# One decoder layer on one core: weights laid out on the host, an earlier attention, 32 expert homes, and a normalisation shared by VectorE and GpSimd

## The reference, cut to what matters

```
x = x + attn(LN(x));  x = x + cross(LN(x), fside, ctx);  x = x + moe(LN(x))
attn:  fused = h @ w_kv_a -> q_c (192), kv_c (64), k_pe (64)
       q = rms(q_c)*gamma @ w_qb -> 16 heads x (128 nope + 64 rope);  kv = rms(kv_c)*gamma @ w_kvb
       scores = q_full @ k_full^T / sqrt(192), causal; softmax; @ v; @ w_o
cross: SmoothQuant int8 linear with fside (256x256), silu(gate)*up, a second one with ctx (256x128)
moe:   sigmoid router, top 3 of 8 groups, top 4 of 32 experts, capacity 40 slots per expert,
       expert = silu(x@Wg)*(x@Wu)@Wd, weighted sum, plus a shared expert
```

## Time and profile before

| what | value |
|---|---|
| median of three runs | 443.41 us |
| the profiled execution's own time | 444.59 us |
| its span, first to last instruction | 442.8 us |
| TensorE busy | 356.5 us (81%) |
| VectorE, GpSimd, ScalarE busy | 249.4, 209.5, 177.0 us |
| granted TensorE clock, mean | 0.938 |
| chain that ended last: PE, DVE, POOL, issue, ACT, DMA | 39, 20, 10, 10, 8, 8% |
| DMA | 32.14 MB in 45512 packets, 44436 of them under 2 KB |

### The profile page before, as it was taken

How to read it: one execution, slowest core, us unless ns; L and a number is a source line. 1 busy time by engine, 2 the same in 40 slices (tenths; PEclk the granted TensorE clock), 3 DMA queues, 4 the chain that set the end, 5 groups by cost and what they waited for, 6 DMA issues and landing times.

```text
span 442.8 us, 7025 instructions
## 1 busy us (share of the span) xinstructions
PE 356.5 (81%) x2206; PEld 250.0 (56%) x2206; DVE 249.4 (56%) x839; ACT 177.0 (40%) x564; POOL 209.5 (47%) x276
## 2 busy tenths in 40 slices
PE   3299989989999998899898895777677652996980
PEld 2154657656677665675665664565565542553870
DVE  2146464575437686877867976662967660336233
ACT  2123447666616865335774236551132000342000
POOL 3102256676718565359976367742134042000674
PEclk9789999999999999999999999899889685998996
DMA  5999508802000000000000000621000004175353
GB/s 158 206 196 283 169 17 227 242 17 71 1 1 1 0 2 1 0 8 28 7 5 3 1 0 7 179 72 38 0 4 2 19 1 125 48 234 177 89 149 114
DMA packets 45512, 32.14 MB, mean 73 GB/s; under 512 B 8697, under 2 KB 44436, under 8 KB 45348
## 3 DMA queue, kind: packets, MB, share of 16 engines
q1 hardware_dynamic: 42980, 28.45, 24.7%
q0 software_dynamic: 2496, 3.25, 2.9%
HBM read 26.56 MB, written 8.84 MB: 80 GB/s over the span
## 4 chain that ended last, share of the span: by engine, by line
PE 39%; DVE 20%; POOL 10%; issue 10%; ACT 8%; DMA 8%; SPq 4%; POOLq 0%; ACTq 0%; DVEq 0%
PE psum L589 29%; PE psum L598 10%; DMA region_b<-in_L_attn_w_o_dram 3%; POOL expert_rows L1685 3%; DMA region_b<-expert_out,slot_gather 2%; POOL region_b L1699 2%; DVE neg_max L1280 2%; POOL region_t L1653 2%; ACT region_r L974 2%; ACT region_t L1035 1%; POOL rstd L1640 1%; DVE smooth L1341 1%; ACT region_t L974 1%; POOL region_t L1652 1%; SPq L496 1%
## 5 line engine op out<-in xcount | busy, mean ns | idle before, releaser
L589 PE MATMUL psum<-region_h,region_b 128*128 128x256 f32 (+1 forms) x352 | 77.5, 354 | 1.7 <-DVE region_b L1592 1.7
L1652 POOL TENSOR_SCALAR region_t<-region_t,prob_rsums 128x128 f32<-128x128 f32 x64 | 40.9, 639 | 52.2 <-DVE prob_rsums L1274 51.7
L1653 POOL TENSOR_SCALAR region_t<-region_t,prob_rsums 128x256 f32<-128x256 f32 x64 | 64.9, 1013 | 0.0
L1033 ACT ACTIVATE region_t<-psum,neg_max 128x128 f32<-128x128 f32 x64 | 23.8, 372 | 94.5 <-DVE neg_max L1280 94.3
L589 PE MATMUL psum<-region_c,region_h 128*128 128x512 f32 x128 | 61.1, 601 | 0.0
L589 PEld LDWEIGHTS psum<-region_h,region_b 128*128 128x128 f32 x352 | 52.4, 193 | 5.9 <-DVE region_b L1592 2.1
L1699 POOL DMA_INDIRECT region_b<-expert_out,slot_gather x20 | 20.7, 1036 | 48.1 <-DMA expert_out<-region_h 42.3
L1685 POOL DMA_INDIRECT expert_rows<-h_moe,slot_scatter x32 | 33.3, 1042 | 18.4 <-DVE slot_scatter L1528 11.4
L598 PE MATMUL psum<-consts,region_t 128*128 128x128 f32 x192 | 32.0, 275 | 10.6 <-ACT region_t L974 9.9
L598 PEld LDWEIGHTS psum<-consts,region_t 128*128 128x128 f32 x192 | 22.3, 141 | 31.8 <-issue 18.4
L1279 DVE TENSOR_REDUCE neg_max<-psum 128x1 f32<-128x128 f32 x64 | 18.1, 282 | 38.8 <-PE psum L589 38.4
(11 more groups left out here) (204 smaller groups left out, 693.1 us busy)
## 6 DMA issues: line engine op xcount, KB each, us to landing
region_a<-in_L_ffn_W_gate_dram SPq DMA_DIRECT2D x17, 128.0 KB, 2.5
region_a<-in_L_ffn_W_up_dram SPq DMA_DIRECT2D x17, 128.0 KB, 2.6
region_a<-in_L_ffn_W_down_dram SPq DMA_DIRECT2D x17, 128.0 KB, 2.7
region_b<-in_L_attn_w_o_dram SPq DMA_DIRECT2D x2, 1024.0 KB, 13.8
expert_out<-region_h SPq DMA_DIRECT2D x8, 256.0 KB, 3.1
expert_rows<-region_g SPq DMA_DIRECT2D x10, 132.5 KB, 4.2
region_b<-in_L_ffn_W_gate_dram SPq DMA_DIRECT2D x10, 128.0 KB, 2.5
region_b<-in_L_ffn_W_up_dram SPq DMA_DIRECT2D x10, 128.0 KB, 2.5
```

The lines of the kernel that those rows point to most:

```text
L589: return nc.tensor.matmul(out_, lhsT, rhs, start=first, stop=last)
L1033: nc.scalar.activation(probs[:, hn % 4, 0:P], s[:, 0:P], ACT.Exp, bias=nmax[:, hn, 0:1], accum_out=sums[:, hn, 0:1])
L1652: g.tensor_scalar(pr[:, 0:P], pr[:, 0:P], rsum[:, hn, 0:1], None, ALU.mult)
L1653: g.tensor_scalar(pr[:, P:3 * P], pr[:, P:3 * P], rsum[:, hn, 1:2], None, ALU.mult).then_inc(sg["probs_normed"], 1)
```

## The change

- The host lays the weights out: per head the transposed blocks and `w_o` side by side (`fold_w`, four quarters of four heads, 9216 bytes a partition), the rope columns (`rope_w`), `fside` and `ctx` transposed, router and shared weights in one array, each expert as one 128 x 768 block; gammas and bias lie in the constants. `prepT`, `rwT`, `shT`, the transposes of `wx`, and their copies go.
- `prepM` writes two banks, (`prepM`) copied by VectorE and (`mo`) by ScalarE, and forms the [P:QL] part twice, one for each half of the partitions. Only pairs 0 and 1 stand ahead of the heads; six stand in slots 0 to 4.
- `q` handles both tiles of a batch: two full matmuls, then two with 64 rows each, on partitions 0-63 and 64-127. There are four q buffers.
- A slot has a single order, `SLOT`; steps in `SPLIT` have a second mark with "*": TensorE works at the first, the other engines at the second. ScalarE's `exp` of head hn-1 stands in slot hn, VectorE's `max` later in the slot. `BANK_PT` and `BANK_Q` are gone; five banks go round.
- VectorE scales tile 0's probabilities, GpSimd tile 1's. One mask matmul of 256 columns takes the place of two of 128.
- All 32 experts have a home and are loaded once, by one DMA each. The two clamps go.

```diff
-BANK_S, BANK_PT, BANK_O, BANK_Q, BANK_W = 0, 2, 3, 4, 5
+BANK_S, BANK_O, BANK_W = 0, 2, 3
...
-EVEN_SLOT = ("scores", 0, "norm", 1, "q", "probsT", 2, "qT", 3)
-ODD_SLOT = ("norm", "scores", "rope", 0, "probsT", 1, "pv", 2, 3)
...
+SLOT = ("scores", "exp", "*pv", "*q", 0, "rope", "probsT", "max", "norm", 1, "*probsT", "qT", "pv", 2, "q", 3, "*qT")
+SPLIT = ("q", "qT", "probsT", "pv", "hT", "fused", "latT", "prepM", "x_T", "x_back", "x_qT", "x_mm",
+         "x_back2", "x_qT2", "x_mm2", "r_T", "r_logit")
...
+PREP_AT = (0, 1, 5, 7, 12, 16)
+FRONT_AT, FRONT_GAPS, FRONT_NEXT = (20, 40, 54), (0, 2, 5, 8), 4
...
+             ("latents", 0), ("prepM", 0), ("latents", 1), ("latT", 0), ("prepM", 1), ("latT", 1), ("q", 0, 0),
+             ("rope", 0, 0), ("rope", 1, 0), ("qT", 0, 0), ("qT", 1, 0)]
+    for p, at in zip(range(2, 8), PREP_AT):
+        place(at, ("prepM", p))
+    place(3, ("q", 0, 1))
+    place(4, ("rope", 0, 1))
+    place(6, ("qT", 0, 1))
+    place(5, ("ln1_stats", 1))
+    place(6, ("ln1_norm", 1))
...
+def tensor_steps(steps):
+    return [step for step in steps if step[0][0] != "*"]
+def other_steps(steps):
+    later = {step for step in steps if step[0][0] == "*"}
+    kept = [step for step in steps if ("*" + step[0],) + step[1:] not in later]
+    return [(step[0].lstrip("*"),) + step[1:] for step in kept]
...
+                for j in range(NJ):
                     k = ring[n % len(ring)]
                     n += 1
+                    self.at[("q", NJ * step[1] + j, step[2])] = (k, emptied[k], filled[k] + 1, emptied[k] + 1)
+                    filled[k] += 1
+                    emptied[k] += 1
...
+        homes = [r[:, o * WE:(o + 1) * WE] for r, n in ((reg_b, SLOTS_B), (reg_a, SLOTS_A), (reg_c, SLOTS_C)) for o in range(n)]
+        homes += [reg_x[:, :], reg_w[:, 0:WE], reg_w[:, WE:2 * WE], reg_g[:, 3328:3328 + WE]]
+        homes += [reg_f[:, o * WE:(o + 1) * WE] for o in range(4)]
...
+            def load_experts(first, n):
+                for e in range(first, first + n):
+                    sp.dma_start(home(e), expert_w[e]).then_inc(ld_experts[e // XG], 16)
...
+            for c in range(NQ):
+                sp.dma_start(fold[c].rearrange("p h m -> p (h m)"), fold_w[c]).then_inc(ld_fold[c], 16)
+                sp.dma_start(wf[:, c, :, HC * KL:], rope_w[c].rearrange("p (k n) -> p k n", k=2)
+                             ).then_inc(ld_rope_cols[c], 16)
+                if c == 1:
+                    load_x(1)
...
+            load_experts(3, 2)
+            load_experts(9, 1)
+            load_experts(SLOTS_B + SLOTS_A + SLOTS_C, 1)
+            for c in range(NQ):
+                for p in range(2 * c, 2 * c + 2):
+                    wait_filled(sp, ("mo", p))
+                load_experts(SLOTS_B + 3 * c if c < 3 else 0, 3)
             wait_filled(sp, ("fused", NT - 1))
-            for e in range(SLOTS_A + 8, SLOTS_A + SLOTS_B):
-                load_expert(e)
+            load_experts(8, 1)
...
+            load_experts(SLOTS_B + SLOTS_A, SLOTS_C)
             sp.wait_ge(sg["scores_ready"], NHU)
-            for e in range(SLOTS_A + 5, SLOTS_A + 8):
-                load_expert(e)
+            load_experts(5, 3)
+            wait_filled(sp, ("y", NT - 1))
+            load_experts(SLOTS_B + SLOTS_A + SLOTS_C + 1, 3)
+            sp.wait_ge(sg["scaledT_w"], B)
+            sp.wait_ge(sg["scaledT_c"], B)
+            load_experts(E - 4, 4)
...
-            for e in range(NHOME, E):
-                if (e - NHOME) % XG == 0:
-                    wait_filled(sp, ("dn", (e - NHOME) // XG))
-                load_expert(e)
-                if (e - NHOME) % XG == XG - 1:
-                    store_outputs((e - NHOME) // XG)
-            for i in range(2, NG_E):
+            for i in range(NG_E):
...
-                    turn(bank(step)[:, 0:P], wq0[:, h, :])
-                    turn(bank(step)[:, P:2 * P], wkq[:, h, 0:DN])
-                    fills(turn(bank(step)[:, 256:320], wkq[0:KL, h, DN:], ident[0:KL, 0:KL]), step)
...
+                        w = fold[p // 2][:, (2 * p + i) % HC, :]
+                        wkT = w[:, QL:QL + KL]
                         mm_halves(bank(step)[:, i * KL:(i + 1) * KL], w[:, 0:P], wkT)
-                        mm(bank(step)[0:64, 128 + i * KL:128 + (i + 1) * KL], w[:, P + KL:2 * P], wkT)
+                        for half in range(2):
+                            last = mm(bank(step)[half * KL:(half + 1) * KL, 128 + i * KL:128 + (i + 1) * KL],
+                                      w[:, P:QL], wkT)
+                    fills(last, step)
+                    item = ("mo", p)
+                    wait_empty(pe, item)
                     for i in range(2):
-                        last = mm(bank(step)[i * KL:(i + 1) * KL, 256:512], wT[:, (2 * p + i) % 4, 256:320], wo[:, 2 * p + i, :])
-                    fills(last, step)
+                        w = fold[p // 2][:, (2 * p + i) % HC, :]
+                        last = mm(bank(item)[i * KL:(i + 1) * KL, 0:D], w[:, QL + KL:QL + 2 * KL], w[:, QL + 2 * KL:])
+                    fills(last, item)
...
+                    for j, item in enumerate(pair):
+                        wait_emptied(pe, ("latT", NJ * b + j))
+                        wait_empty(pe, item)
+                        mm(bank(item), qn0[:, NJ * b + j, :], wf[:, c, 0, :], True, False)
+                    for j, item in enumerate(pair):
+                        half = slice(j * KL, (j + 1) * KL)
+                        fills(mm(bank(item), qn1[half, b, :], wf[half, c, 1, :], False, True), item)
...
-                    mm(o[:, 0:P], id_bf[:], mask_bf[:], True, False)
-                    mm(o[:, 0:P], q[:, 0:P], kT[:, b, 0:P], False, True)
-                    mm(o[:, P:3 * P], q[:, P:2 * P], kT[:, b, :], True, False)
-                    mm(o[:, 2 * P:3 * P], id_bf[:], mask_bf[:], False, True).then_inc(sg["scores_ready"], 1)
+                    mm(o[:, 0:2 * P], id_bf[:], mask_bf[:], True, True)
+                    nc.tensor.matmul(o[:, 0:P], q[:, 0:P], kT[:, b, P:2 * P], start=False, stop=True,
+                                     skip_group_check=True)
+                    nc.tensor.matmul(o[:, P:3 * P], q[:, P:2 * P], kT[:, b, :], start=False, stop=True,
+                                     skip_group_check=True).then_inc(sg["scores_ready"], 1)
...
+                    pe.wait_ge(sg["probs0_normed"], hn + 1)
                     pe.wait_ge(sg["probs_normed"], hn + 1)
-                    if hn >= 1:
-                        pe.wait_ge(sg["probsT_copied"], hn)
-                    for i in range(3):
-                        last = turn(ps_pt[:, i * P:(i + 1) * P], probs[:, hn % 4, i * P:(i + 1) * P])
-                    last.then_inc(sg["probsT_done"], 1)
+                    wait_empty(pe, step)
+                    for i, block_ in enumerate((0, 2, 1)):
+                        last = turn(bank(step)[:, i * P:(i + 1) * P], probs[:, hn % 4, block_ * P:(block_ + 1) * P])
+                    fills(last, step)
...
-                elif kind == "scores":
+                elif kind == "exp":
                     hn, = a
                     act.wait_ge(sg["max_ready"], hn + 1)
                     if hn >= 4:
-                        act.wait_ge(sg["probsT_done"], hn - 3)
+                        wait_filled(act, ("probsT", hn - 4))
...
-                    link(v.tensor_scalar(qa, qa, QMAX, -QMAX, ALU.min, ALU.max))
...
-                    link(v.tensor_scalar(fa, fa, QMAX, -QMAX, ALU.min, ALU.max))
...
+                    dve.wait_ge(sg["rsum_ready"], hn + 1)
+                    pr = probs[:, hn % 4, :]
+                    v.tensor_scalar(pr[:, 0:P], pr[:, 0:P], rsum[:, hn, 0:1], None, ALU.mult
+                                    ).then_inc(sg["probs0_normed"], 1)
+                elif kind == "max":
...
-                    g.tensor_scalar(pr[:, 0:P], pr[:, 0:P], rsum[:, hn, 0:1], None, ALU.mult)
...
+    heads = np.concatenate([qb[:, :, 0:DN].transpose(1, 2, 0), kvb[:, :, 0:DN].transpose(1, 2, 0),
+                            kvb[:, :, DN:].transpose(1, 2, 0), wo], axis=2)
+    fold_w = heads.reshape(NQ, HC, P, FW).transpose(0, 2, 1, 3).reshape(NQ, P, HC * FW)
+    pe = qb[:, :, DN:].reshape(QL, NQ, HC * DR).transpose(1, 0, 2)
+    rope_w = np.concatenate([pe[:, 0:P], np.concatenate([pe[:, P:QL], pe[:, P:QL]], axis=1)], axis=2)
+    side = a["fside_BxS2xS2_0"].transpose(2, 0, 1).reshape(KD, P, B, D).transpose(1, 2, 0, 3).reshape(P, B * 2 * D)
...
+    experts = np.concatenate([np.concatenate([gate, up], axis=3).reshape(E, P, 2 * KD * I), a["L0_ffn_W_down"]], axis=2)
```

More of the change, by code:

```diff
@@ L147, in plan @@
     for b in range(B):
[L148 removed]
+        place(4 * NH * b + (WX_AT if b else WX_FIRST), ("wx", b))
         if b == B - 1:
@@ L601, in bf @@
                 return bank(item).bitcast(BF16)
-            for step in steps:
+            for step in steps_te:
                 kind, a = step[0], step[1:]
@@ L705, in _ @@
```

(3 more changed lines are left out.)

430 lines of the change are left out of this document (168 added, 262 removed), and 1 row of the table ITEMS.

## The result

The changed kernel takes 423.9 us (423.2 to 425.2, four runs) where the kernel before takes 442.7 (441.0 to 449.0) on the same chip: ratio 0.959, 95% interval 0.955 to 0.963. Faster, as forecast, but by 19 us instead of 43. The time lies at the very end of the range (378 to 424) and outside the likeliest case's own (390 to 408). The profiled execution took 424.1 us, its span 422.3.

The account below looks back on a forecast made before the run. The heads were taken as bound by TensorE, loosely in the last two batches. From 444.6 us: start -17, heads -21, chain -1.3, experts -4.1 give 401.2, less 1.2 for the median: 400 us, range 378 to 424.

Parts of the forecast that it names:

- likeliest case: Whole kernel: the forecast itself, 400 us, with its own range of 390 to 408; chance 0.44.
- Start: Ahead of the heads: first mask near 27.5 us instead of 44.66, a gain of 17 us, range 13 to 19.
- Heads: The 64 heads: 250.1 us would become 229.5, 21 less.
- 13.0 us of TensorE's work: In the heads: paired q -11.2 us, transposes that go -5.5, more prepM +3.7, mask 0; together -13.0.
- 10.6 us of idleness ahead of the probability transposes: In the heads: TensorE's wait behind ScalarE's copy from the only bank goes with five banks and a later exp, -10.6 us.
- VectorE was put at +3: In the heads: tile 0's multiplications load VectorE; a late copy or maximum of its adds 3 us on TensorE.
- Rival 2: In the heads: VectorE becomes the bound through the lock with GpSimd, 0.89 us a head; 413 us, 408 to 430; chance 0.16.
- Rival 3: In q: the row halves run one after another and drain TensorE; 418 us; chance 0.08.
- Rival 4: In the heads: the loop over two score banks sets the pace and makes the kernel slower, 453 us; chance 0.03.
- Rival 1: In the heads: the new order frees all 23.1 us of TensorE idleness, without VectorE's price; 385 us, 376 to 390; chance 0.25.
- Chain behind the heads: Cross block and router behind the heads: the two clamps go, 0.83 + 0.42 us, -1.3.
- Experts: Expert stage: with all experts at home the wait for reloads and the lower clock after it go, -4.1 us.

Follow-up runs that it names:

- the best version: Changed kernel with prepM 2 to 7 ahead of the heads and tile 0's normalisation back on GpSimd: 413.8 us, 0.932 of the kernel before.

## Why the prediction was half right

**Start: right, -19 for -17.** The first mask came at 25.55 us instead of 44.66; 27.5 was predicted. q started at 17.02 (18.1 predicted). The prediction's steps from q to the mask add to 25.9 and not to 26.3; that changes nothing. The timeline of the changed kernel:

```profile
14.70 0.70 POOL L1605 TENSOR_TENSOR rrms<-rms_eps,neg_half 128x2 f32<-128x2 f32 x1
...
17.02 3.17 PE L600 MATMUL psum<-region_c,region_h 128*128 128x512 f32 x8
...
21.69 0.84 POOL L1617 TENSOR_TENSOR q_chunk<-q_chunk,q_rope_tmp 128x256 f32<-128x256 f32 x1 [6.28 <-DVE q_chunk L1231]
...
25.55 0.37 PE L600 MATMUL psum<-mask_bf,ident_bf 128*128 128x256 bf16 x1 [0.78 <-ACT region_b L961]
```

The doubt about the first quarter fell to the good side: the start moved 356 GB/s, where the earlier trace rows had 156 and 240, and nothing waited for a weight.

**Heads: wrong, +0.6 for -21; this is the step that failed.** Its line is "250.1 - 13.0 - 10.6 + 3 = 229.5". Term by term:

- Of the 13.0 us of TensorE's work 11.5 went, by busy time, the q pair at 2.87 us instead of 2.58. What failed is that they were put on the path. From the earlier trace rows I read a TensorE busy for 59 of 62 us as the bound; but its order is fixed and each head's scores wait for an exponential two heads back. Taking work away elsewhere makes TensorE reach that wait sooner. The run without the mask gives a seventh to a third; by that rate, which is an estimate for other places, 13 us are worth 2 to 4. The rate is not the same in both directions nor everywhere: putting the row halves back cost 0.6 of their size (0.7 in batch 1), and batch 0's folding all of it.
- The 10.6 us of idleness ahead of the probability transposes went, but the heads did not get shorter by them: TensorE's idleness in all rose, from 23.1 to 34.8 us. This term failed with the first. The run with the exponential in its own slot is 13.4 us longer, but 1.3 shorter in the batch at equal clock, so it does not give the term's price.
- VectorE was put at +3 and costs 10.4; GpSimd was given nothing and gives back 3.8. The multiplication itself is cheaper than I took it (0.4), as its median in this line of the changed kernel shows:

```profile
L1241 DVE TENSOR_SCALAR region_t<-region_t,prob_rsums x64: 285/286/1283, 36.5 to 281.1; 128x128 f32<-128x128 f32 x64
```

Busy time was 21.2 us, 0.33 a head. The price of it was what I had wrong: not "a copy or a maximum of VectorE's" that is late now and then, but half its size on the whole and a third of it even in batch 1 (1.8 of 4.9), where VectorE is busy for 36.6 of 56.6 us. An engine two thirds busy is not free when three engines pass each head on in order.
- The folding in batch 0 had its TensorE time in the sum, +3.7 for three more `prepM`, and that was about right: batch 0 grew by 4.4 us while the other three shrank by 3.8 together. Moving all six out takes 7.3 us off batch 0 for 7.6 of TensorE's busy time. What the sum missed is that this cost is paid in full, where the savings elsewhere are worth a fraction of their size.

What the failed terms are worth together can be read from one run, without adding single edits. With tile 0's multiplication back on GpSimd, and everything else in place, the heads take 242.9 us, 6.0 less than before the change. So of the 13.0 + 10.6 = 23.6 us of the TensorE terms 6.0 came, 17.6 too few. Moving the multiplication cost 6.6 (10.4 on VectorE, of which GpSimd gives back 3.8) for 3, 3.6 too many. 17.6 + 3.6 = 21.2 is the distance from -20.6 to +0.6. The second part was shown by moving the work and by leaving it out. For the first, the run without the mask shows that TensorE's work counts for little; which step of the loop of scores, maximum and exponential comes last was not isolated, and how the 6.0 us divide between the two TensorE terms isn't known.

Two more slips: the likeliest case's own range was given as 390 to 408, though its terms (start 4 less to 2 more, heads 4 either way) make it 394 to 408; and VectorE's time in the third batch, put at 53.4 us, was 49.4.

**Rivals.** Rival 2 had the engine right and the mechanism wrong. The Trainium skill ("SBUF — State Buffer", Who interferes with whom) lets a VectorE operation wait for a whole GpSimd one. The trace agrees where the two meet: three multiplications began 0.07 to 0.09 us into a rope addition of GpSimd, with 0.63 to 0.64 us of it left, and took 0.71 to 0.73. But 58 of the 64 took 0.285 to 0.289 us, and only five more than 0.7. GpSimd's own multiplication, released by the same reciprocal, never ran when VectorE's began; 19 of the 24 that began beside a rope addition did so in its last 0.18 us and lost nothing. Above 0.286 a piece, all 64 together lost 2.9 us. So the cost was order and not the port. Rival 3 is refuted by the full rows, though a drain is there: the pair is 0.29 us above 2.58. The Trainium skill ("TensorEngine Tiling (Array Packing)", Key Properties) has TensorE drain on a change of tiling mode. The trace agrees for two thirds of it: 0.09 to 0.10 us are lost where the halves begin and again where they end, but as much between their two passes, where the mode does not change. Rival 4's loop did not decide by itself: its waits are 5.5 of TensorE's 34.8 idle us. Rival 1 is refuted.

**Chain behind the heads: -0.7 for -1.3**, from the last head's maximum to the first transpose of the expert rows. (Counted by the first and last maxima, -18.4, +0.6, -0.7 and -2.0 add up to the span's -20.5.) **Experts: -2.0 for -4.1.** The stall is gone and the last eviction ends 30.7 + 0.6 us behind the stage's start instead of 34.5 + 0.6: -3.8, near the -4.1. But the last store then took 3.89 us where it had taken 2.14, and the gathers wait for it. From the chain of waits of the changed kernel:

```profile
385.58 0.61 ACT region_h L961
386.19 0.02 issue
386.20 3.89 DMA expert_out<-region_h
...
390.99 0.34 POOL region_b L1657
```

and of the kernel before:

```profile
407.86 0.61 ACT region_h L974
408.46 0.02 issue
408.48 2.14 DMA expert_out<-region_h
...
411.51 0.34 POOL region_b L1699
```

In thirteen of the experiments the chain names that store: it took 3.8 to 4.2 us in twelve and 2.40 in one (the best version). What goes with it is a second transfer. In the changed kernel a packet of the queue that the profile calls instruction, 16 KB and 1.09 us long, starts 1.39 us into the store. DMA from 386 to 390.2 us in the changed kernel:

```profile
q1 hardware_dynamic: 544, 0.52, 37.9%
q8 instruction: 1, 0.02, 1.6%
expert_out<-region_h SPq DMA_DIRECT2D x1, 256.0 KB, 3.9
```

and from 386 to 388.6 us in the run without the mask, the same store:

```profile
q1 hardware_dynamic: 544, 0.52, 61.2%
expert_out<-region_h SPq DMA_DIRECT2D x1, 256.0 KB, 2.1
```

Such a packet starts 1.05 to 1.39 us into the last store in each of the thirteen traces in which that took 3.8 to 4.2 us. In the kernel before it starts 2.01 us into it and costs nothing; in the run without the mask and in the one with q ahead of qT and the normalisation on GpSimd none starts there, and the store takes 2.14 and 2.15; in the best version it falls into the sixth store, which then takes 3.47. By these traces the 1.75 us depend on where such a packet falls and are not a price of the new layout; no run moved the packet on purpose.

## What to carry to other kernels

A TensorE that is busy for 91% of a stage (here the heads of the kernel before) is not proof that TensorE is the bound: where each engine's order is written out and heads pass through a loop of four engines, a cut of one engine's work counts only at a place where that engine is what the others wait for. Price each engine by leaving out a small, even share of its work (here the mask, here the normalisation) before a large change is built on it, and compare stretches at the same granted clock; a large wait may be slack, as the 30.5 us ahead of rope were. And when work is moved out of the start, look at the batch in which it lands as a term of its own.
